# Layer 2's last row tiles multiplied from idle buffers, products five steps behind the scores, 16 dummy matmuls in place of 24

## The chip, the cores and the metric

One Trainium2 chip, one of its cores. The metric is device time of one launch in microseconds (us). Engines: PE (TensorE, matmuls), DVE (VectorE), ACT (ScalarE), POOL (GpSimd) and SP (SyncE, here the queue that issues every DMA).

## What is computed

Four graph-attention layers on x (16 batch elements, 1024 nodes, 64 features) with one adjacency matrix per element; each layer is followed by `x = layernorm(x + layer(x))`. Layer 2, whose end the change touches, has 8 heads:

```
scores = einsum('bmhd,bnhd->bhmn', q, k) * scale + edge_bias[edges]
scores = leaky_relu(scores, 0.2), masked where edges == 0
attn   = softmax(scores, axis=-1)
out    = einsum('bhmn,bnhd->bmhd', attn, v) @ Wp + bp
```

Layer 3 scores a pair of nodes by `a . leaky_relu(u_i + v_j)` over 64 features, then softmax, product and ELU.

## The kernel before

Each engine runs its own hand-written program; semaphores alone order them. The outer loop (`Fori`) has one turn per batch element g: layer 3 of element g, with layers 0 and 1 of element g+1 woven in (`ahead`), then layer 2 of element g+1. So there are 16 ends of layer 2; 15 of them are followed by a layer 3 that has the next element's work in it.

Layer 2 runs 4 pairs of heads x 8 row tiles = 32 steps `s`, two tiles `n = 2s, 2s+1` (one per head) a step, 64 tiles in all. For a tile, PE makes 128x1024 scores (`scores`), ACT applies a ReLU, DVE combines to the leaky ReLU and takes a minimum (`leaky`, L1243), ACT takes the exponential. The result must be transposed before it can be multiplied. For 15 of the 16 quads (a quad is 4 tiles, 2 steps, number `k`) DVE transposes 32x32 blocks within partitions (L1271) into one of two buffers `blocks`, and SP issues 16 DMAs (`move`, L380) that carry the blocks across partitions into one of three buffers `quadT`. `pv_quad(k, part)` (L697) then multiplies half a quad, `LAG = 3` quads behind the scores, so at steps 2k+6 and 2k+7. The last quad (tiles 60 to 63) isn't moved: PE transposes its tiles into PSUM (`turn`, L522) and DVE copies them out (L1276) into a `blocks` buffer, whose last content must have been moved first. Between these, PE also makes the next pair's queries (`q`), values (`vw`) and transposes the last pair's result (`heads`); all of these share the PSUM space `turn`, one at a time, in the order of `extra_use`. DVE multiplies a pair's turned heads by the inverse row sums (`pair_out`, L1284) and POOL adds them up.

When the last pair's products are done, ACT copies them (L959), PE turns them (`turn_heads`), and DVE, after its loop has closed, adds, normalises and writes `x2`. PE meanwhile closes its loop, makes two products for the next element (`first_products`, L527 and L544), issues `KEEP = 24` dummy matmuls (L776), then turns x2 and makes layer 3's columns and values. ACT makes `ucol` in two halves (L1021, L1022). Layer 3's main loop starts with the first matmul of L808. POOL converts the next element's adjacency rows from `adj_in` into `mask_next` during layer 2.

## Time and profile before

| | us |
|---|---|
| median of 3 runs | 9054.23 (9046.0 to 9068.25) |
| the profiled execution's own time | 9052.68 |
| its span | 9050.9 |
| PE, DVE, ACT, POOL busy | 90%, 82%, 78%, 16% of the span |
| mean granted TensorE clock | 0.958 of full |

Times in the rows are microseconds from the span's start. A row of the timeline merges like instructions that follow each other; in brackets stands the engine's idle time before them and what ended it. A clock of 1.00 is 2.4 GHz, 0.50 is 1.2 GHz. One turn of the loop takes some 553 us: the dummies of one end of layer 2 start at 3226.27, those of the next at 3780.78.

### The profile page before, as it was taken

The page shows a single profiled execution, that of the slowest core. Times are in us where ns is not written, and L with a number is a line of the kernel's source. Part 1 is how long each engine was busy: PE and PEld are TensorE (multiplying, and loading weights), DVE is VectorE, ACT ScalarE, POOL GpSimd, SP SyncE. Part 2 cuts the span into 40 slices and gives each one's busy share as a digit, 9 for nine tenths or more (in the row PEclk, how much of TensorE's full clock was granted, in tenths as well). Part 3 has the DMA queues.
Part 4 walks back from the last instruction along what each step waited for, and adds up shares of the span by engine and source line. Part 5 has one row for each costly group of instructions (what it writes and reads, how often), then busy time and mean ns, then how long its engine had stood idle before and what let it go on. Part 6 is the DMA issues. An engine that isn't in the chain of part 4 may idle for free.

```text
span 9050.9 us, 165102 instructions
## 1 busy us (share of the span) xinstructions
PE 8158.5 (90%) x57976; PEld 3621.5 (40%) x57976; DVE 7394.6 (82%) x11173; ACT 7034.4 (78%) x8220; POOL 1429.1 (16%) x582
## 2 busy tenths in 40 slices
PE   3899998989999899998998989899898998999999
PEld 1434435343353433434334353443534435343352
DVE  3788787987879878798787978878788787987878
ACT  2788786977869778787787878778688786977877
POOL 0301203021030301203012030120302103021000
PEclk7999999999999999999999999999999999999999
DMA  2715426253362623527145271542715426253251
GB/s 72 159 35 114 101 50 155 42 129 80 66 139 50 144 58 78 129 46 165 37 100 112 47 167 35 114 98 53 155 39 120 91 49 155 44 132 75 56 126 19
DMA packets 2150347, 822.58 MB, mean 91 GB/s; under 512 B 1146914, under 2 KB 2129954, under 8 KB 2147362
## 3 DMA queue, kind: packets, MB, share of 16 engines
q1 hardware_dynamic: 2149410, 810.76, 40.9%
q8 instruction: 507, 8.31, 0.4%
q14 instruction: 430, 3.52, 0.1%
HBM read 76.25 MB, written 4.19 MB: 9 GB/s over the span
## 4 chain that ended last, share of the span: by engine, by line
PE 36%; SPq 21%; DVE 18%; issue 13%; ACT 8%; DMA 3%; DVEq 0%; POOL 0%; ACTq 0%; POOLq 0%
SPq L380 20%; PE psum L808 19%; DVE work L1379 6%; ACT work L1035 5%; PE psum L527 3%; PE psum L697 3%; DVE work L1271 3%; DVE work L1243 3%; PE psum L599 2%; PE psum L522 2%; PE psum L544 1%; PE psum L776 1%; DMA work<-work 1%; PE psum L669 1%; ACT spare L877 1%
## 5 line engine op out<-in xcount | busy, mean ns | idle before, releaser
L808 PE MATMUL psum<-work,pick 128*32 128x512 f32 x32768 | 3758.0, 598 | 198.1 <-DVE work L1379 162.2
L1035 ACT ACTIVATE work<-spare,ucol 128x1024 f32<-128x1024 f32 x3402 | 3633.7, 1147 | 52.0 <-PE psum L808 48.6
L1379 DVE TENSOR_SCALAR work<-spare,ucol 128x1024 f32<-128x1024 f32 x4790 | 3250.2, 745 | 305.8 <-ACT ucol L1022 233.7
L808 PEld LDWEIGHTS psum<-work,pick 128*32 128x32 f32 x32768 | 975.9, 110 | 2532.0 <-issue 2065.5
L944 ACT ACTIVATE work<-psum,beta 128x1024 f32<-128x1024 f32 x1024 | 1138.9, 1112 | 474.0 <-PE psum L669 395.6
L1271 DVE STREAM_TRANSPOSE work<-work 128x1024 f32<-128x1024 f32 x960 | 1191.1, 1241 | 295.3 <-DMA work<-work 177.1
L1243 DVE CUSTOM_DVE_ANT_0 work<-psum,work 128x1024 f32<-128x1024 f32 x1024 | 1225.7, 1197 | 155.0 <-ACT work L944 143.6
L951 ACT ACTIVATE work<-work,least 128x1024 f32<-128x1024 f32 x1024 | 1172.2, 1145 | 54.7 <-DVE least L1243 54.5
L665 PE MATMUL psum<-mask,ident_b 128*128 128x512 bf16 x2048 | 643.5, 397 | 304.3 <-DVE least L1243 301.0
L1460 POOL TENSOR_TENSOR rstd<-rstd,neg_half 128x8 f32<-128x8 f32 x64 | 131.6, 2056 | 4951.5 <-DVE rstd L1182 4951.5
L669 PE MATMUL psum<-x_split,q_hi 128*128 128x512 f32 x2048 | 862.0, 503 | 0.0
L697 PE MATMUL psum<-work,vw 128*64 128x256 f32 x5632 | 701.7, 393 | 0.0
L669 PE MATMUL psum<-x_split,q_lo 128*128 128x512 f32 x2048 | 660.2, 404 | 0.0
L1438 POOL TENSOR_SCALAR mask_next<-adj_in 128x1024 bf16<-128x1024 int32 x120 | 436.4, 3637 | 442.8 <-DMA adj_in<-in_adj 434.7
L697 PEld LDWEIGHTS psum<-work,vw 128*64 128x64 f32 x5632 | 384.4, 140 | 285.6 <-issue 130.2
L669 PEld LDWEIGHTS psum<-x_split,q_hi 128*128 128x128 f32 x2048 | 405.1, 198 | 159.9 <-issue 15.5
L1440 POOL TENSOR_SCALAR no_edge<-adj_in 128x1024 bf16<-128x1024 int32 x120 | 436.1, 3634 | 9.5
L669 PEld LDWEIGHTS psum<-x_split,q_lo 128*128 128x128 f32 x2048 | 398.1, 194 | 92.3
L1146 DVE CUSTOM_DVE_ANT_0 spare<-psum,spare 128x1024 f32<-128x1024 f32 x256 | 311.2, 1216 | 110.5 <-ACT spare L872 107.3
L665 PEld LDWEIGHTS psum<-mask,ident_b 128*128 128x128 bf16 x2048 | 125.2, 99 | 688.3 <-DVE least L1243 524.0
L872 ACT ACTIVATE spare<-psum,sbias 128x1024 f32<-128x1024 f32 x256 | 284.4, 1111 | 91.2 <-PE psum L582 77.9
L599 PE MATMUL psum<-q_lo,vw 128*64 128x256 f32 x2048 | 262.9, 401 | 67.3 <-DMA q_lo<-spare 37.1
(161 smaller groups left out, 6985.1 us busy)
## 6 DMA issues: line engine op xcount, KB each, us to landing
work<-work SPq DMA_DIRECT2D x2560, 128.0 KB, 2.5
spare<-work SPq DMA_DIRECT2D x1280, 128.0 KB, 2.5
adj_in<-in_adj SPq DMA_DIRECT2D x128, 512.0 KB, 4.9
q_lo<-adj_in SPq DMA_DIRECT2D x1024, 64.0 KB, 2.1
q_lo<-spare SPq DMA_DIRECT2D x1024, 64.0 KB, 2.1
work<-work SPq DMA_DIRECT2D x1792, 32.0 KB, 1.9
mask<-mask_next SPq DMA_DIRECT2D x16, 2048.0 KB, 9.3
x_in<-in_x SPq DMA_DIRECT2D x16, 256.0 KB, 9.6
```

Source lines behind the costliest of these rows:

```text
L380: sp.dma_start(dst[32 * c:32 * c + 32, :, a, :], src[32 * a:32 * a + 32, :, c, :]).then_inc(done, 16)
L599: mm = pe.matmul(dst, values[layer][:, j, :], src[:, j, :, :, :], start=(j < 2), stop=(j >= NT - 2))
L665: pe.matmul(slot[:, cols], ident_b[:], mask[:, t, cols], start=True, stop=False)
L669: mm = pe.matmul(slot[:, cols], left, x_split[:, cols], start=False, stop=(k == 1))
L697: mm = pe.matmul(dst, vw[:, pair % 2, j, F * h:F * h + F], src[:, j, :, h, :].rearrange("p a (t i) -> p a t i", t=2), start=(j == 0), stop ...
L808: mm = pe.matmul(slot[32 * q:32 * q + 32, cols], pick[:, 15 - kk:47 - kk], ring[kk % 4][q][:, cols], start=False, stop=(kk == 15), skip_gr ...
L944: act.activation(probs[n % 4], score[n % 2], ACT.Relu, bias=beta4[:, t, 2 * pair + h:2 * pair + h + 1], scale=GAIN[2]).then_inc(s_relu, 1)
L951: act.activation(probs[n % 4], probs[n % 4], ACT.Exp, bias=least[:, n % 4:n % 4 + 1], scale=-1.0, accum_out=rowsum[:, pair % 2, 2 * t + h: ...
L1035: ins = act.activation(ring[kk % 4][q], v3, ACT.Relu, bias=ucol[:, 4 * T + q, kk:kk + 1])
L1243: dve.tensor_tensor_reduce(probs[n % 4], score[n % 2], probs[n % 4], -ALPHA[2], 3.0e38, ALU.add, ALU.min, least[:, n % 4:n % 4 + 1]).then_ ...
L1271: dve.transpose(dst[:, :, h, half, :], probs[n % 4].rearrange("p (b j) -> p b j", j=32))\
L1379: ins = dve.tensor_scalar(ring[kk % 4][q], v3, ucol[:, 4 * T + q, kk:kk + 1], 0.0, ALU.add, ALU.max)
```

## The change

Six edits, all around the end of layer 2:

1. The last four tiles go to two idle places instead of a `blocks` buffer: tiles 60 and 61 into `adj_in` (after POOL has converted the last adjacency rows), tiles 62 and 63 into the first half of a `quadT` buffer (after quad 12's products). They are multiplied one row tile at a time (`pv_last`), the first before quad 14, the second after it.
2. `LAG` becomes 5 steps: `pv_quad(k, part)` runs at steps 2k+5 and 2k+6, one step earlier. `heads` moves from t=7 to t=6, `vw` from t=6 to t=5, the copies of the heads from t=2 and 6 to t=1 and 5.
3. `KEEP` goes from 24 to 16 dummies.
4. DVE's last `pair_out` is taken out of the branch at the end of layer 2 and stands at the start of `layer3`, behind the loop's end.
5. DVE writes x2 before the next element's column correction (`column_low`), not after it.
6. DVE makes one half of `ucol`, ACT the other. The queue of POOL gets one semaphore increment for the last element.

```diff
-LAG = 3
+LAG = 5
-KEEP = 24
+KEEP = 16
...
+        last_rows = [adj_in[:].rearrange("p a b -> p (a b)").bitcast(F32),
+                     work[:, 4:6, :].rearrange("p a b -> p (a b)")]
...
+            def pv_last(it, half):
+                in_sbuf(pe, it, ("tile", TILES2 - 3 + 2 * half))
+                src = last_rows[half].rearrange("p (b a h i) -> p b a h i", a=4, h=2, i=32)
+                cols = slice((NT - 2 + half) * P, (NT - 1 + half) * P)
+                for j in range(NT):
+                    for h in range(2):
+                        mm = pe.matmul(outT[F * h:F * h + F, cols], vw[:, (HP - 1) % 2, j, F * h:F * h + F],
+                                       src[:, j, :, h, :], start=(j == 0), stop=(j == NT - 1))
...
-                    if s >= 2 * LAG:
-                        pv_quad(g, it, s // 2 - LAG, s % 2, tail)
+                    if s >= LAG:
+                        pv_quad(g, it, (s - LAG) // 2, (s - LAG) % 2, tail)
...
-                pv_quad(g, it, QUADS - 3, 1, tail)
-                for k in (QUADS - 2, QUADS - 1):
-                    pv_quad(g, it, k, 0, tail)
-                    pv_quad(g, it, k, 1, tail)
+                pv_quad(g, it, MOVED - 2, 0, tail)
+                turn_tile(g, it, TILES2 - 2)
+                pv_quad(g, it, MOVED - 2, 1, tail)
+                turn_tile(g, it, TILES2 - 1)
+                pv_last(it, 0)
+                pv_quad(g, it, MOVED - 1, 0, tail)
+                pv_quad(g, it, MOVED - 1, 1, tail)
+                pv_last(it, 1)
                 turn_heads(g, it, HP - 1)
...
+                if h == 0 and half == 0:
+                    dve.wait_ge(s_mask_next, g + 2)
+                if h == 0 and half == 1:
+                    dve.wait_ge(s_pv, g * QUADS + MOVED - 2)
...
-                pair_out(g, it, HP - 1)
```

PE at the end of layer 2, before. `ident,work` is a tile turned, `ident,heads_T` a pair's heads turned, `work,vw` and `spare,vw` products of a quad (x8 is half a quad):

```order
L697 MATMUL psum<-work,vw 64x4x2x32 x8
L522 MATMUL psum<-ident,work 128x128 x8
L665 MATMUL psum<-mask,ident_b 128x512 x2
L669 MATMUL psum<-x_split,q_hi 128x512 x2
L669 MATMUL psum<-x_split,q_lo 128x512 x2
L522 MATMUL psum<-ident,work 128x128 x8
L522 MATMUL psum<-ident,heads_T 128x128 x8
L697 MATMUL psum<-work,vw 64x4x2x32 x8
L522 MATMUL psum<-ident,work 128x128 x8
L697 MATMUL psum<-work,vw 64x4x2x32 x8
L522 MATMUL psum<-ident,work 128x128 x8
L697 MATMUL psum<-work,vw 64x4x2x32 x8
L697 MATMUL psum<-spare,vw 64x4x2x32 x16
L697 MATMUL psum<-work,vw 64x4x2x32 x16
L522 MATMUL psum<-ident,heads_T 128x128 x8
```

And PE there now:

```order
L523 MATMUL psum<-ident,heads_T 128x128 x8
L695 MATMUL psum<-work,vw 64x4x2x32 x8
L523 MATMUL psum<-ident,work 128x128 x8
L666 MATMUL psum<-mask,ident_b 128x512 x2
L670 MATMUL psum<-x_split,q_hi 128x512 x2
L670 MATMUL psum<-x_split,q_lo 128x512 x2
L523 MATMUL psum<-ident,work 128x128 x8
L695 MATMUL psum<-work,vw 64x4x2x32 x8
L523 MATMUL psum<-ident,work 128x128 x8
L695 MATMUL psum<-work,vw 64x4x2x32 x8
L523 MATMUL psum<-ident,work 128x128 x8
L708 MATMUL psum<-adj_in,vw 64x128 x16
L695 MATMUL psum<-spare,vw 64x4x2x32 x16
L708 MATMUL psum<-work,vw 64x128 x16
L523 MATMUL psum<-ident,heads_T 128x128 x8
```

The third pair's heads and the second half of quad 12 now stand ahead of the last scores, and half of the last quad's product stands ahead of quad 14's.

DVE from the last `leaky` to the loop's end and behind it, before:

```order
L1276 COPY work<-psum 128x32x32 [waits s_turned,s_quad_moved1]
L1243 ISA work,least<-psum,work 128x1024 [waits s_relu]
L1243 ISA least 128x1
L1276 COPY work<-psum 128x32x32 [waits s_turned]
L1280 RECIPROCAL rinv<-rowsum 128x16
L1284 TENSOR_TENSOR heads_T<-psum,rinv 128x1024 [waits s_turned,s_acc,s_vec]
L1276 COPY work<-psum 128x32x32 [waits s_turned] x2
L1280 RECIPROCAL rinv<-rowsum 128x16
L1284 TENSOR_TENSOR heads_T<-psum,rinv 128x1024 [waits s_turned,s_acc,s_vec]
L1326 UNCONDITIONAL_BRANCH
L1397 UNCONDITIONAL_BRANCH
```

And now:

```order
L1288 COPY adj_in<-psum 128x32x32 [waits s_turned,s_mask_next]
L1251 ISA work,least<-psum,work 128x1024 [waits s_relu]
L1251 ISA least 128x1
L1288 COPY adj_in<-psum 128x32x32 [waits s_turned]
L1288 COPY work<-psum 128x32x32 [waits s_turned,s_pv]
L1288 COPY work<-psum 128x32x32 [waits s_turned]
L1340 UNCONDITIONAL_BRANCH
L1418 UNCONDITIONAL_BRANCH
L1375 RECIPROCAL rinv<-rowsum 128x16
L1074 ISA
L1376 ISA [waits s_vec]
```

The wait for quad 13's move became waits for the mask and for a product, and the last multiplication stands behind both branches.

## Rows read from the trace of the kernel before

**Rows 1.** The page, part 4: chain that ended last, by engine, by line.
```profile
PE 36%; SPq 21%; DVE 18%; issue 13%; ACT 8%; DMA 3%; DVEq 0%; POOL 0%; ACTq 0%; POOLq 0%
SPq L380 20%; PE psum L808 19%; DVE work L1379 6%; ACT work L1035 5%; PE psum L527 3%; PE psum L697 3%; DVE work L1271 3%; DVE work L1243 3%; PE psum L599 2%; PE psum L522 2%; PE psum L544 1%; PE psum L776 1%; DMA work<-work 1%; PE psum L669 1%; ACT spare L877 1%
```

**Rows 2.** Groups of instructions, all stretches: busy, mean ns | idle, releasers.
```profile
L1271 DVE STREAM_TRANSPOSE work<-work 128x1024 f32<-128x1024 f32 x960 | 1191.1, 1241 | 295.3 <-DMA work<-work 177.1 <-DMA spare<-work 117.7
```

**Rows 3.** Timeline, PE, an end of layer 2: start us, us, engine line op.
```profile
3194.50 1.09 PE L522 MATMUL psum<-ident,work 128*128 128x128 f32 x8 [2.41 <-DVE work L1276]
3196.99 1.96 PE L522 MATMUL psum<-ident,heads_T 128*128 128x128 f32 x8 [1.39 <-DVE work L1276]
...
3207.03 3.62 PE L697 MATMUL psum<-spare,vw 128*64 128x256 f32 x32
3210.49 3.62 PE L697 MATMUL psum<-work,vw 128*64 128x256 f32 x32
3214.80 1.09 PE L522 MATMUL psum<-ident,heads_T 128*128 128x128 f32 x8 [0.70 <-ACT heads_T L959]
```

**Rows 4.** Timeline, SP, the same end: quad 14's 16 DMA issues.
```profile
3190.21 11.55 SPq L380 DMA_DIRECT2D spare<-work  x16
```

**Rows 5.** Line L380 from 3125 to 3206 us.
```profile
DMA to landing us min/median/max: 2.3/2.8/4.4
```

**Rows 6.** Timeline, SP and PE, the ends with the longest and shortest gap.
```profile
6519.04 10.51 SPq L380 DMA_DIRECT2D spare<-work  x16
...
6537.93 3.62 PE L697 MATMUL psum<-spare,vw 128*64 128x256 f32 x32
...
7637.22 11.64 SPq L380 DMA_DIRECT2D spare<-work  x16
...
7651.19 3.62 PE L697 MATMUL psum<-spare,vw 128*64 128x256 f32 x32
```

**Rows 7.** Timeline, PE, layer 3: products of 64 weights with 128 columns.
```profile
3323.08 1.09 PE L762 MATMUL psum<-work,vw 128*64 128x128 f32 x16
```

**Rows 8.** Timeline, DVE, around the same end.
```profile
3193.22 1.22 DVE L1276 COPY work<-psum 128x1024 f32<-128x1024 f32 x1 [2.35 <-DMA work<-work]
...
3219.19 1.42 DVE L1364 TENSOR_TENSOR za<-za,heads_T 128x512 f32<-128x512 f32 x2 [2.03 <-issue]
...
3225.38 0.76 DVE L1188 TENSOR_TENSOR x<-zb,rstd 128x256 f32<-128x256 f32 x2
3242.95 4.73 DVE L1379 TENSOR_SCALAR work<-spare,ucol 128x1024 f32<-128x1024 f32 x7 [16.80 <-ACT ucol L1022]
```

**Rows 9.** Timeline, POOL: the last mask rows of the next element.
```profile
3180.02 2.14 POOL L1443 TENSOR_TENSOR mask_next<-mask_next,no_edge 128x1024 bf16<-128x1024 bf16 x1
```

**Rows 10.** Timeline, PE, from the loop's end to layer 3's first matmuls.
```profile
3219.26 3.77 PE L527 MATMUL psum<-xT_in,WD 64*128 64x512 f32 x4 [3.36 <-issue]
...
3226.27 7.57 PE L776 MATMUL psum<-mask,ident_b 128*128 128x512 bf16 x24
3233.68 1.04 PE L522 MATMUL psum<-ident,x 128*64 128x128 f32 x8
...
3249.31 2.87 PE L808 MATMUL psum<-work,pick 128*32 128x512 f32 x16
```

**Rows 11.** The same at the next end of layer 2.
```profile
3787.43 1.04 PE L522 MATMUL psum<-ident,x 128*64 128x128 f32 x8
...
3798.05 1.92 PE L808 MATMUL psum<-work,pick 128*32 128x512 f32 x16 [0.54 <-ACT work L1035]
```

**Rows 12.** Stretches at the first end: busy of PE, PEld, DVE, ACT, POOL, granted clock, DMA.
```profile
3226.00:3230.00 4.00, 4.00 (x11) 1.50 (x11) 0.14 (x1) 0.67 (x2) 0.00 (x0) 0.50 0.00 0
3230.00:3234.00 4.00, 4.00 (x19) 1.91 (x18) 0.00 (x0) 0.00 (x0) 0.00 (x0) 0.90 0.00 0
```

**Rows 13.** One stretch behind x2's transposes at each of 15 ends: first and last.
```profile
478.00:483.00 5.00, 5.00 (x24) 2.99 (x23) 1.76 (x3) 3.91 (x5) 0.00 (x0) 1.00 0.00 0
...
8239.00:8244.00 5.00, 5.00 (x17) 3.45 (x16) 1.01 (x2) 1.67 (x3) 0.00 (x0) 0.50 0.00 0
```

More of the change, by code:

```diff
@@ L64, in extra_use @@
     pair, t = divmod(s, NT)
-    if t == 7 and pair:
+    if t == 6 and pair:
         return ("heads", pair - 1)
     if pair + 1 < HP:
-        return {3: ("q", 2 * pair + 2), 4: ("q", 2 * pair + 3), 6: ("vw", pair + 1)}.get(t)
+        return {3: ("q", 2 * pair + 2), 4: ("q", 2 * pair + 3), 5: ("vw", pair + 1)}.get(t)
     return None
@@ L712, in layer2 @@
                 scores(g, it, 1, tail)
-                for s in range(STEPS2):
-                    pair, t = divmod(s, NT)
+                for s in range(STEPS2 - 1):
                     n = 2 * s
-                    more = s + 1 < STEPS2
                     extra = extra_use(s)
-                    if more:
-                        scores(g, it, n + 2, tail)
+                    scores(g, it, n + 2, tail)
                     if extra:
@@ L985, in layer2 @@
                         elu3(tail)
-                    if t == 2 and pair:
+                    if t == 1 and pair:
                         copy_out(g, pair - 1, 0)
-                    if t == 6 and pair:
+                    if t == 5 and pair:
                         copy_out(g, pair - 1, 1)
@@ L1264, in turn_tile @@
                 k, half, h, moved = in_quad(n)
-                if k >= 2 and half == 0 and h == 0:
+                if moved and k >= 2 and half == 0 and h == 0:
                     dve.wait_ge(s_moved[(k - 2) % 4],
```

51 lines of the change are left out of this document (28 added, 23 removed).

## The prediction

> **What bounds the kernel now.** The chain of work that ended last has PE first and SP's queue second: L380, the DMA issues of layer 2's moves, is 20% of the span, and L808, layer 3's main loop, 19% [rows 1]. So two regimes alternate. In layer 2 the chain runs through SP: 16 issues take 11.6 us for a quad [rows 4], and DVE stood 295 us before its transposes, nearly all of it for a move to land [rows 2]. In layer 3 PE, ACT and DVE are all loaded. Between them, once per batch element, lies a stretch in which one engine at a time works, and the change is about that. The timeline of PE there shows it: the last tile transposes with waits of 2.41 and 1.39 us, quad 14's product at 3207.03, the last quad's at 3210.49, the heads at 3214.80 [rows 3], the loop's end 3.36 us, two products, 24 dummies in 7.57 us, x2's transposes at 3233.68 and the first matmul of layer 3 at 3249.31 [rows 10]. DVE has x2 ready at 3226.1 (3225.38 + 0.76) [rows 8], 7.5 us before PE turns it. From the heads to layer 3, PE is the chain and DVE waits.
>
> **Earlier start and shorter end of the last products.** Quad 14's last DMA is issued at about 3201.1 (3190.21 + 11.55 less one issue of 0.65) [rows 4] and lands some 2.8 us later [rows 5], say 3203.8. PE starts its product at 3207.03 [rows 3], 3.3 us late. The change takes from PE between tile 61's transposes and that product: the heads with their wait (1.39 + 1.89) and the second half of quad 12 (2.45, what lies between the heads and the next transposes), and adds the first `pv_last`. Its price is bounded by two rows: 16 records with 64 weights and 128 columns took 1.09 us [rows 7], it has 32, so 2.1 us at most without overlap; half a quad with as many columns is 1.8 (3.62 / 2) [rows 3]. I take 1.95. So 12.53 - 3.28 - 2.45 + 1.95 = 8.75 us behind 3194.50, PE is ready at 3203.3, about when the move lands. The start at 3194.50 itself should hold: the copy of tile 60 no longer waits 2.35 us for quad 13's move [rows 8], while the third pair's multiplication (1.2 us and a reciprocal of 0.24) now stands ahead of it. Behind quad 14's product stands 1.95 us of work in place of 3.5, so 1.5 us more.
>
> The gap between landing and product differs: taken the same way at all 16 ends it lies between 0.4 us (7651.19) and 6.4 us (6537.93) [rows 6], mean 3.5. I take off 0.5 for ends at which PE isn't ready at the landing. 3.5 - 0.5 + 1.5 = 4.5 us, x 16 = **72 us**. Bounds: 1.5 (24 us in all, if PE is never earlier) and 5.0 (80 us).
>
> The new waits are covered: the mask that tile 60's copy waits for was done at 3182.2 [rows 9], 11 us before that copy; behind the copy on DVE stand the last `leaky` and the other copies, so it would matter at once if POOL came later. The wait for quad 12's product is met, since that product now stands before tile 60's transposes on PE.
>
> **Products one step earlier in the loop.** A step is about 6 us (half of the 11.6 us of SP's issues for a quad [rows 4]), so every product starts that much sooner behind its move. I take the worse case, that this uses up the slack and PE waits for some landings, and cost it at nothing still: DVE waits in the same step for the same landing before its transposes [rows 2], and the scores that stand behind the product on PE need a `leaky` that stands behind a transpose of 1.24 us; transpose and `leaky` are 2.4 us, the half quad 1.9. SP's order and its DMAs don't change, POOL's queue gets its heads a step sooner and has time for them. Bounds: 0 and, in a rival below, a slip of each quad.
>
> **Dummies.** 24 take 7.57 us [rows 10]; the clock was 0.50 until 3230 and then full [rows 12], so some 9 run at 0.43 us each and 15 in the remaining 3.6, 0.21 to 0.24 each. Eight fewer at full clock are 1.7 us, and PE is the chain there, since x2 is ready long before: also in the change, where PE would come to the transposes at least 15 us behind the heads and DVE needs 10.2 (3215.9 to 3226.1). 16 x 1.7 = **27 us**. At half clock they would be 3.4 us each end; nothing if DVE were late.
>
> **What the clock does behind the dummies.** At 15 ends I asked for the granted clock in a stretch just behind x2's transposes: 8 have 1.00, 7 have 0.50 [rows 13]. Where it fell, x2's transposes to layer 3's first matmul took 15.6 us (3233.68 to 3249.31) and its first 16 records 2.87 [rows 10]; where it didn't, 10.6 us and 1.92 [rows 11]. A fall costs 5.0 + 0.95, about 6 us. PE has dense dummies, then 1.04 us of transposes, 1.2 us idle and dense products. In the end with a fall the clock had been full for 3.5 us when the dummies ended; with 8 fewer it is full for about 1.8 us. The sparse stretch then comes sooner behind the rise, with the products right behind it. No row shows this spacing. I estimate that 5 of the 7 falls go: 5 x 6 = **30 us**. Bounds: none goes (0), and all go (42 us), or 8 new ones come, below.
> The Trainium skill (TensorE: Matmul & The Clock Gate, part 4) says that transposes on PE don't count as busy for the clock; by it the sparse stretch is longer than the rows of PE suggest, and fewer dummies would be the wrong direction. The rows don't tell transposes from idle time.
>
> **What hangs on nothing.** Moving `pair_out` behind the loop's end takes away DVE's 2.03 us between multiplication and additions [rows 8], and x2 before the column correction another 1.2, but both end at x2, which waits for PE. Half of `ucol` on DVE starts DVE's ring tiles 0.7 us earlier than 3242.95 [rows 8], but PE's first ring matmul came at 3249.31 behind its own products, or 0.54 us behind ACT [rows 11], which must copy the values first. All three: 0.
>
> **Sum.** The profiled execution's own time is 9052.7, 1.5 us under the median. 9052.7 - 72 - 27 - 30 = **8924 us**, 1.4% faster.
>
> **The rivals.**
> - *The falls stay.* Fewer dummies shift them but as many remain: 9052.7 - 72 - 27 = 8954. For it: 7 of 15 is near a coin's toss, and what decides isn't visible in the rows.
> - *The last products stay late.* PE isn't ready at the landing, because the turned tiles go back and forth between PE and DVE and the third pair's heads now precede them: only 1.5 us of the 4.5. 9052.7 - 24 - 27 - 30 = 8972. Against it: the sum above, which has PE ready 0.5 us before the landing.
> - *Too few dummies to raise the clock.* It stays at half through transposes and products: 8 ends more pay 6 us (+48), 15 pay 0.9 in the transposes (+14), the dummies give nothing. 9052.7 - 72 + 62 = 9043, no difference. Against it: the clock rose some 4 us into the dummies [rows 12], and 16 at half clock last 6.8. The rule "transposes don't count" above would point here too.
> - *Products in the loop wait and hold the scores.* If each quad's blocks come w later because PE stood for a landing, SP starts later, and the chain is SP's: 15 quads x 16 x w = 240 w. With w = 1 it is 8924 + 240 = 9164; it decides from w = 0.54, and is slower by over 0.3% from 0.65. Against it: DVE waits for the same landings, and a late product only touches tiles three quads on.
> - *More than the sum.* All 7 falls go and PE is ready at every landing: 80 + 27 + 42 = 149, 8904; if PE, fed more evenly, also has fewer of its short falls inside layer 2, a little less: 8900.
>
> **How the numbers follow.** Forecast 8924: 0.48. Falls stay (8954): 0.20. Last products stay late (8972): 0.09. Clock stays at half (9043): 0.05. Loop slips: 0.08, of which 0.05 above 9081. Even faster (8900): 0.10. The range 8885 to 8980 takes in the forecast with its bounds (8903 with 80, 27 and 42), the even faster case and the first two rivals, and leaves out 0.13 and tails. About 0.3% (27 us) is what a measurement of this kernel can tell from no change. Faster by more: 0.87. Within it: 0.08. Slower by more: 0.05.
>
> **What would show it.** Right: quad 14's product within 1 us of its landing, heads some 6 us behind that landing, 16 dummies in 5 to 6 us with the clock rising among them, at most 3 of 15 stretches at 0.50, PE still waiting for nothing but "issue" at the loop's end. Wrong: PE waits before L695 for DMAs longer than DVE does before its transposes, a longer time from the first `leaky` to the last than now, or clocks of 0.50 in the products behind x2.

## The result: 0.6% faster, not 1.4%

Measured: 9010.28 us median of 5 runs (8996.97 to 9021.64) against 9061.8 of the kernel before on the same chip (5 runs, 9046.0 to 9070.84). The ratio is 0.9943, 95% interval 0.9926 to 0.9959. The forecast was 8924, its range 8885 to 8980: the direction was right, the time 86 us too low and outside the range. Of the 129 us forecast, 51.5 came. The profiled execution of the changed kernel took 9021.64 (span 9019.7), the slowest of the five.

Both traces were cut at the same points in all 16 turns and the stretches summed. "Loop" is from the first `leaky` of an element to the landing of quad 14, "late" from that landing to quad 14's product, and the last two stretches part at the end of the sixteenth matmul of layer 3's main loop. For the kernel before I give the same sums from its trace.

| Sum over 16 elements, us | before | after | difference | forecast |
|---|---|---|---|---|
| loop | 3181.6 | 3249.6 | +68.0 | 0 |
| late | 56.0 | 2.2 | -53.8 | -48 (3.0 x 16) |
| quad 14's product to heads | 124.5 | 99.5 | -25.0 | -24 (1.5 x 16) |
| heads to x2's transposes (dummies in it) | 272.8 | 244.8 | -28.0 | -27 |
| x2's transposes to layer 3's 16th matmul | 251.1 | 259.0 | +7.9 | -30 |
| rest of layer 3 and what is woven in | 4899.1 | 4899.9 | +0.8 | 0 |

With -1.0 ahead of the first element that is -31.2, the difference of the spans (rounding apart). Three of the terms came as forecast. Two did not: the loop, 68 us, and the falls of the granted clock behind x2's transposes, 38 us (+7.9 where -30 was forecast).

What the chain that ended last says now, page part 4, by engine and by line (answers [rows 1]):

```profile
PE 38%; SPq 23%; DVE 15%; issue 13%; ACT 9%; DMA 1%; DVEq 0%; POOL 0%; ACTq 0%; POOLq 0%
```

PE and SP's queue have each gained 2 points, DVE has lost 3 and DMA 2. Groups of instructions, all stretches (busy, mean ns | idle before them, releasers), for DVE's `leaky` and block transposes, then products of quads on PE:

```profile
L1251 DVE CUSTOM_DVE_ANT_0 work<-psum,work 128x1024 f32<-128x1024 f32 x1024 | 1227.0, 1198 | 247.1 <-ACT work L953 237.4
L1279 DVE STREAM_TRANSPOSE work<-work 128x1024 f32<-128x1024 f32 x960 | 1190.9, 1240 | 263.3 <-DMA work<-work 168.7
...
L695 PE MATMUL psum<-work,vw 128*64 128x256 f32 x5120 | 641.4, 394 | 21.0 <-DMA work<-work 20.8
...
L695 PE MATMUL psum<-spare,vw 128*64 128x256 f32 x2560 | 312.6, 389 | 66.5 <-DMA spare<-work 66.5
```

The transposes wait 263 us, 32 less than in [rows 2]. PE now waits 87 us for landings ahead of its products, where it waited for none before. But the row to look at is the first. `leaky` stood 155.0 us before, 143.6 of them behind ACT's ReLU, in this line of the page of the kernel before:

```profile
L1243 DVE CUSTOM_DVE_ANT_0 work<-psum,work 128x1024 f32<-128x1024 f32 x1024 | 1225.7, 1197 | 155.0 <-ACT work L944 143.6
```

Now it stands 247.1. These 92 us are DVE waiting for ACT's ReLU, which comes as late as its scores do.

**The end of layer 2 did what was forecast.** Timeline of PE, changed kernel, the same end as [rows 3] and [rows 10] (start us, us, engine, line; in brackets the idle time before and what ended it):

```profile
3195.40 1.97 PE L708 MATMUL psum<-adj_in,vw 128*64 128x128 f32 x32
3199.31 3.67 PE L695 MATMUL psum<-spare,vw 128*64 128x256 f32 x32 [1.94 <-DMA spare<-work]
3202.78 1.95 PE L708 MATMUL psum<-work,vw 128*64 128x128 f32 x32
3205.41 1.09 PE L523 MATMUL psum<-ident,heads_T 128*128 128x128 f32 x8 [0.69 <-ACT heads_T L968]
3209.79 3.77 PE L528 MATMUL psum<-xT_in,WD 64*128 64x512 f32 x4 [3.28 <-issue]
...
3216.80 4.99 PE L784 MATMUL psum<-mask,ident_b 128*128 128x512 bf16 x16
3221.63 1.04 PE L523 MATMUL psum<-ident,x 128*64 128x128 f32 x8
3223.86 4.64 PE L528 MATMUL psum<-xTa,G 65*128 65x512 f32 x8 [1.20 <-ACT xTa L1025]
3228.30 3.52 PE L545 MATMUL psum<-linT_s,xTa 65*128 65x64 f32 x16
...
3236.41 3.64 PE L817 MATMUL psum<-work,pick 128*32 128x512 f32 x16
```

PE waits 1.94 us for quad 14 to land and starts its product with the landing; the estimate for half of the last quad (1.95) is measured as 1.97 and 1.95. The heads come 6.1 us behind the product's start where they took 7.8 [rows 3], and 16 dummies last 4.99 us where 24 took 7.57. A landing still takes about as long as before, 2.4 us in the median where [rows 5] has 2.8; line L381 from 3120 to 3204 us:

```profile
DMA to landing us min/median/max: 2.3/2.4/4.1
```

DVE's rows at that end, timeline: a copy into an idle place, `pair_out`'s reciprocal behind the loop's end, x2, and the first ring tiles:

```profile
3186.36 1.23 DVE L1288 COPY adj_in<-psum 128x1024 f32<-128x1024 f32 x1
...
3198.78 0.25 DVE L1375 RECIPROCAL rinv<-rowsum 128x16 f32<-128x16 f32 x1 [2.05 <-issue]
...
3213.45 0.76 DVE L1196 TENSOR_TENSOR x<-zb,rstd 128x256 f32<-128x256 f32 x2 [1.55 <-POOL rstd L1481]
...
3229.53 4.73 DVE L1400 TENSOR_SCALAR work<-spare,ucol 128x1024 f32<-128x1024 f32 x7 [0.23 <-DVE ucol L1388]
```

The copy into `adj_in` has no wait where its counterpart in [rows 8] waited 2.35 us, and the wait for the mask is met: POOL's last mask row ended at 3176.4. x2 is ready at 3214.2, 7.4 us ahead of its transposes (3221.63). So 16 dummies still cover DVE, and PE is the chain.

**The loss is in the loop, once per element.** Times from an element's first `leaky`, medians of 14 elements, show where:

| | quad 1 | quad 2 | quad 3 | quad 7 | quad 14 |
|---|---|---|---|---|---|
| SP starts its DMAs, before | 29.0 | 44.2 | 56.3 | 104.7 | 187.0 |
| after | 29.0 | 48.9 | 60.4 | 108.1 | 191.0 |

Up to quad 1 the two are alike; quad 2 starts 4.7 us late, and what follows carries it without growing. Summed over all 16 elements, the time from quad 1's first DMA to quad 2's is 308.0 us after and 240.6 before. These 67.4 us are as much as the whole loop lost; its other parts differ by up to 11 us either way and cancel. In the element with no layer 3 beside it (the first) quad 2 starts 0.9 us later, and quad 14 1.3 us earlier.

Timeline of PE in the changed kernel, one of step 4's scores and step 5 of one element:

```profile
3025.07 0.60 PE L666 MATMUL psum<-mask,ident_b 128*128 128x512 bf16 x2
...
3030.61 0.60 PE L666 MATMUL psum<-mask,ident_b 128*128 128x512 bf16 x2 [4.02 <-DVE least L1251]
...
3032.06 3.62 PE L565 MATMUL psum<-Cv,xTa 65*128 65x128 f32 x16
3035.61 3.45 PE L695 MATMUL psum<-work,vw 128*64 128x256 f32 x16
3038.99 0.61 PE L666 MATMUL psum<-mask,ident_b 128*128 128x512 bf16 x2
```

L565 is `vw(1)`, the second pair's values, and L695 the first product, quad 0's. Both now fall into step 5. PE has just stood 4.02 us, because DVE normalises layer 3's result there. The stretches of the same time (us, then busy and count of PE, PEld, DVE, ACT, POOL, granted clock, DMA share, GB/s) show the clock behind that pause:

```profile
3026.00:3030.60 4.60, 0.59 (x3) 0.16 (x1) 4.20 (x22) 3.00 (x5) 2.03 (x2) 1.00 0.66 148
3030.60:3032.00 1.40, 1.39 (x6) 1.08 (x7) 1.40 (x2) 1.23 (x2) 1.32 (x2) 0.95 0.88 204
3032.00:3035.60 3.60, 3.60 (x17) 3.32 (x15) 3.60 (x6) 1.11 (x1) 3.60 (x1) 0.50 0.89 200
3035.60:3039.00 3.40, 3.40 (x18) 1.74 (x18) 2.46 (x4) 2.15 (x3) 3.32 (x1) 0.55 0.56 128
```

The clock falls to 1.2 GHz behind the pause, and the two products run at it: 3.62 and 3.45 us instead of 1.95 each. The next scores come 7 us later, and DVE runs dry:

```profile
3036.82 1.24 DVE L1279 STREAM_TRANSPOSE work<-work 128x1024 f32<-128x1024 f32 x1
3041.82 1.23 DVE L1251 CUSTOM_DVE_ANT_0 work<-psum,work 128x1024 f32<-128x1024 f32 x1 [3.76 <-ACT work L953]
```

In the kernel before, PE pauses 3.10 us at this place and the clock falls too, but step 5 has only scores to make at 1.2 GHz. Both pieces stand at step 6, at 2.4 GHz. The pause in the timeline of PE, then stretches (columns as above), then the two pieces:

```profile
3036.06 0.89 PE L665 MATMUL psum<-mask,ident_b 128*128 128x512 bf16 x2 [3.10 <-DVE least L1243]
```

```profile
3036.00:3042.00 6.00, 5.13 (x12) 2.92 (x12) 6.00 (x8) 3.48 (x5) 5.84 (x4) 0.52 0.86 196
...
3044.00:3048.00 4.00, 4.00 (x35) 2.97 (x34) 4.00 (x6) 3.42 (x5) 3.73 (x3) 1.00 0.18 41
```

```profile
3044.09 1.95 PE L564 MATMUL psum<-Cv,xTa 65*128 65x128 f32 x16
3045.96 1.95 PE L697 MATMUL psum<-work,vw 128*64 128x256 f32 x16
```

That the pause is what brings the clock down is not shown: no run shortened it or put dummies into it.

### The profile page after: what moved, and what is told of

The parts are those of the page before. It is cut to its first block, busy times and chain, and to the rows that moved or that the text cites. A ratio compares the mean times of both kernels' runs of the same rounds, so it can differ in the third digit from the quotient of the medians.

```text
span 9019.7 us, 165963 instructions
## 1 busy us (share of the span) xinstructions
PE 8145.7 (90%) x58360; PEld 3645.7 (40%) x58360; DVE 7407.4 (82%) x11189; ACT 7012.7 (78%) x8204; POOL 1428.7 (16%) x582
## 4 chain that ended last, share of the span: by engine, by line
PE 38%; SPq 23%; DVE 15%; issue 13%; ACT 9%; DMA 1%; DVEq 0%; POOL 0%; ACTq 0%; POOLq 0%
SPq L381 22%; PE psum L817 21%; DVE work L1400 6%; ACT work L1043 5%; PE psum L528 3%; PE psum L600 3%; PE psum L695 2%; DVE work L1279 2%; PE psum L670 1%; DVE work L1251 1%; PE psum L523 1%; PE psum L545 1%; ACT spare L886 1%; ACT spare L881 1%; PE psum L784 1%
## 5 line engine op out<-in xcount | busy, mean ns | idle before, releaser
L817 PE MATMUL psum<-work,pick 128*32 128x512 f32 x32768 | 3766.7, 599 | 192.1 <-DVE work L1400 161.5
L817 PEld LDWEIGHTS psum<-work,pick 128*32 128x32 f32 x32768 | 977.8, 110 | 2531.4 <-issue 2069.1
L1251 DVE CUSTOM_DVE_ANT_0 work<-psum,work 128x1024 f32<-128x1024 f32 x1024 | 1227.0, 1198 | 247.1 <-ACT work L953 237.4
L695 PE MATMUL psum<-work,vw 128*64 128x256 f32 x5120 | 641.4, 394 | 21.0 <-DMA work<-work 20.8
L695 PEld LDWEIGHTS psum<-work,vw 128*64 128x64 f32 x5120 | 348.0, 140 | 292.8 <-issue 114.1
L695 PE MATMUL psum<-spare,vw 128*64 128x256 f32 x2560 | 312.6, 389 | 66.5 <-DMA spare<-work 66.5
```

Of the source, the lines that this page charges most:

```text
L695: mm = pe.matmul(dst, vw[:, pair % 2, j, F * h:F * h + F], src[:, j, :, h, :].rearrange("p a (t i) -> p a t i", t=2), start=(j == 0), stop ...
L817: mm = pe.matmul(slot[32 * q:32 * q + 32, cols], pick[:, 15 - kk:47 - kk], ring[kk % 4][q][:, cols], start=False, stop=(kk == 15), skip_gr ...
L1251: dve.tensor_tensor_reduce(probs[n % 4], score[n % 2], probs[n % 4], -ALPHA[2], 3.0e38, ALU.add, ALU.min, least[:, n % 4:n % 4 + 1]).then_ ...
```

## The experiments

The theory is that the loop loses because `vw(1)` and quad 0's product stand in the one step where PE comes out of a pause at 1.2 GHz. Its rivals are that the products, being earlier, wait for landings in every quad, or that the tail or DVE's edits do it. For the second miss the question is whether the falls stayed, moved or were paid elsewhere. All kernels had the kernel before run beside them on their chip; every difference below is the median's to that one. The sums are those of the first table, one trace for each kernel. The kernel before had medians of 9061.8, 9076.45 (beside e1 to e4), 9062.34 (e5 to e8) and 9081.5 (e9 to e12), so a difference of a few us between sums of different traces can be the chip's.

| | kernel | median | difference | ratio and interval | loop | late | product to x2's transposes | to 16th matmul |
|---|---|---|---|---|---|---|---|---|
| | before (first trace) | | | | 3181.6 | 56.0 | 397.3 | 251.1 |
| | after | 9010.28 | -51.5 | 0.9943, 0.9926 to 0.9959 | 3249.6 | 2.2 | 344.3 | 259.0 |
| e1 | after, `vw(1)` at step 6 | 8970.74 | -105.7 | 0.9878, 0.9857 to 0.9898 | 3197.1 | 3.0 | 354.2 | 249.5 |
| e2 | before, products a step earlier | 9044.30 | -32.2 | 0.9965, 0.9951 to 0.998 | 3220.9 | 2.2 | 412.5 | 256.1 |
| e3 | after, 24 dummies | 9044.37 | -32.1 | 0.996, 0.9943 to 0.9977 | 3245.1 | 3.1 | 379.7 | 257.6 |
| e4 | after, DVE's edits undone | 9016.27 | -60.2 | 0.9935, 0.9918 to 0.9952 | 3237.9 | 2.8 | 350.0 | 252.9 |
| e5 | after, products at the old steps | 8989.61 | -72.7 | 0.9918, 0.9901 to 0.9935 | 3173.2 | 53.7 | 344.7 | 248.2 |
| e6 | before, 16 dummies | 9003.36 | -59.0 | 0.9933, 0.9916 to 0.995 | 3190.1 | 27.3 | 375.5 | 234.1 |
| e7 | e1 with 5 dummies behind x2's transposes | 8942.69 | -119.7 | 0.9866, 0.9846 to 0.9887 | 3195.6 | 2.5 | 344.9 | 232.6 |
| e8 | e1 with 8 dummies | 8957.16 | -105.2 | 0.9885, 0.9866 to 0.9904 | 3181.1 | 2.4 | 315.0 | 273.4 |
| e9 | e5 with `vw(1)` at step 5 | 9018.30 | -63.2 | 0.9933, 0.9916 to 0.9949 | 3208.4 | 53.2 | 346.5 | 252.8 |
| e10 | before with 5 behind | 9035.55 | -46.0 | 0.9955, 0.9938 to 0.9972 | 3186.6 | 39.6 | 400.3 | 223.9 |
| e11 | e1 with 8 dummies, 5 behind | 8913.27 | -168.2 | 0.9827, 0.9809 to 0.9844 | 3189.4 | 2.5 | 319.3 | 222.8 |
| e12 | e1 with 8 dummies, 10 behind | 8917.60 | -163.9 | 0.9823, 0.9807 to 0.984 | 3189.1 | 2.2 | 315.9 | 233.2 |

**e1: one number in the table of steps.**

```diff
-        return {3: ("q", 2 * pair + 2), 4: ("q", 2 * pair + 3), 5: ("vw", pair + 1)}.get(t)
+        return {3: ("q", 2 * pair + 2), 4: ("q", 2 * pair + 3), 5 if pair else 6: ("vw", pair + 1)}.get(t)
```

> The changed kernel with one thing put back: in the first pair of heads, PE makes the next pair's values (vw) at step 6 again instead of step 5. Theory A (the loop lost 61.6 us over 16 elements because at step 5 of an element PE has vw and the first half quad's product in a row, straight behind the wait for DVE's layer-3 normalisation, so that the scores behind them come late): quad 2's first DMA comes back from 48.9 to about 44.5 us behind the element's first leaky, the loop's 16 stretches fall from 3111 to about 3050 us, and the time is 50 to 60 us less than the change, near 8955. Rival B (the products one step earlier wait for landings in every quad, and the values have nothing to do with it): quad 2 stays near 49, the time stays within 15 us of the change, 8995 to 9025.

The loop's sum falls by 52.5 us, the time by about 54 (105.7 less 51.5), and quad 2's DMAs start at 45.4. Products five steps behind stay as they are, so landings in every quad are not the cause of these 54 us. PE at step 5 and 6 in this kernel, timeline:

```profile
3018.12 0.61 PE L666 MATMUL psum<-mask,ident_b 128*128 128x512 bf16 x2 [4.03 <-DVE least L1251]
...
3019.70 3.46 PE L695 MATMUL psum<-work,vw 128*64 128x256 f32 x16
...
3025.85 1.95 PE L565 MATMUL psum<-Cv,xTa 65*128 65x128 f32 x16
3027.72 1.95 PE L695 MATMUL psum<-work,vw 128*64 128x256 f32 x16
```

The pause and the product at 1.2 GHz are still there. `vw(1)`, one step later, takes 1.95.

**e5: the tail without the earlier products.**

```diff
-LAG = 5
+LAG = 6
-    if t == 6 and pair:
+    if t == 7 and pair:
...
-        return {3: ("q", 2 * pair + 2), 4: ("q", 2 * pair + 3), 5: ("vw", pair + 1)}.get(t)
+        return {3: ("q", 2 * pair + 2), 4: ("q", 2 * pair + 3), 6: ("vw", pair + 1)}.get(t)
...
+                turn_heads(g, it, HP - 2)
+                pv_quad(g, it, MOVED - 3, 1, tail)
+                turn_tile(g, it, TILES2 - 2)
                 pv_quad(g, it, MOVED - 2, 0, tail)
-                turn_tile(g, it, TILES2 - 2)
...
```

> The kernel before's loop (products six steps behind, vw at step 6, heads at step 7) with the change's end of layer 2, its 16 dummies and DVE's part; the third pair's heads and the second half of quad 12 stay behind the last scores. The run of the loop's part alone had brought quad 14's product to its landing already (2.2 us of lateness in 16 ends, before 56) and cost 49 us in the loop. So, theory D: most of the 54 us that quad 14's product came earlier is the loop's edit, not the idle buffers. Then here the loop's stretches are about 3050 us, quad 14's product stays 30 us or more late in sum, the heads follow it 6.2 us later, and the time lies near the step-6 run or up to 20 us above it, ratio to before 0.988 to 0.991. Rival E: the idle buffers alone (no wait for quad 13's move) bring quad 14's product to its landing; then lateness is under 10 us and the ratio is 0.985 to 0.988.

It is 72.7 us faster than before. The whole change has 51.5; the intervals overlap (0.9901 to 0.9935, 0.9926 to 0.9959), so that the change without its earlier products is the faster is likely and not shown. The loop's loss is gone (3173.2, 76 under after), quad 2's DMAs start at 44.4, and quad 14's product is late again by 53.7. So the earlier start of quad 14's product and the loop's loss both belong to the earlier products, and the 53 us ahead of x2's transposes to the tail and the dummies.

**e9: `vw(1)` alone at step 5**, the edit against e5. With e1 and e5 this completes a table of two by two. Its columns differ in more than the first product: all products, the heads and the heads' copies are a step earlier on the right, and the third pair's heads and half of quad 12 stand ahead of the last scores there.

```diff
-        return {3: ("q", 2 * pair + 2), 4: ("q", 2 * pair + 3), 6: ("vw", pair + 1)}.get(t)
+        return {3: ("q", 2 * pair + 2), 4: ("q", 2 * pair + 3), 6 if pair else 5: ("vw", pair + 1)}.get(t)
```

> Tail-only kernel (products six steps behind, `heads` and `vw` of before) with one move: the second pair's values, `vw(1)`, at step 5 in place of 6. The fourth cell of a table: vw at 6 with products at 6 (8989.6), vw at 6 with products at 5 (e1, loop sum 3058.9), both at 5 (after, 3111.2). Theory A, each piece of PE work at step 5 delays quad 2 by its own length (1.95 us at full clock, more at half): 15 elements x 1.9 to 2.5 = 29 to 38 us, about 9022, loop sum about 3055. Rival B, only the pair of them in a row overruns DVE's slack: 8990. Rival C, the values alone do all of it: some 9040, quad 2's issues start 4.5 us later as in after.

| loop; start of quad 2's DMAs | products from step 6 | products from step 5 |
|---|---|---|
| `vw(1)` at 6 | 3173.2; 44.4 (e5) | 3197.1; 45.4 (e1) |
| `vw(1)` at 5 | 3208.4; 46.8 (e9) | 3249.6; 48.9 (after) |

By these sums `vw(1)` alone costs 35 us, the products alone 24, both together 76. But they run to quad 14's landing and hold the end of layer 2 as well, and they scatter: e6 and e10 have the loop of the upper left cell and measure 3190.1 and 3186.6; e7, e8, e11 and e12 have that of the upper right one and lie between 3181.1 and 3195.6. Cut at the place itself, the cells hardly scatter:

| from quad 1's first DMA to quad 2's, summed over 16 elements | products from step 6 | products from step 5 |
|---|---|---|
| `vw(1)` at 6 | 240.6 to 241.6 (before, e5, e6, e10) | 250.7 to 254.8 (e1, e7, e8, e11, e12) |
| `vw(1)` at 5 | 273.2 (e9) | 292.4 to 308.0 (after, e2, e3, e4) |

There the product alone costs 9 to 14 us, `vw(1)` alone 32, both 51 to 67, more than their sum. That would follow if DVE had slack in step 5 that is used up only once, which no run tests by itself. Theory A, that each piece costs its own length, holds in the trace for `vw(1)`: the loop up to the last `leaky`, the sum meant in the expectation, is 3056.9 where e5 has 3023.6. In the times it is not so plain: e9 is 29 us above e5 as measured, but only 9.5 when each is taken against the kernel before on its own chip, and their intervals overlap (0.9901 to 0.9935, 0.9916 to 0.9949). So the lone `vw(1)` rests on the trace, and the move of e1, 54 us, on times too.

The clock's part can be read inside the four traces that have both at step 5. In 14 of their 60 elements behind the first, the clock fell later: `vw(1)` took 2.06 to 2.83 us, and quad 2 started 17.2 to 17.5 us behind quad 1. In the other 46 it took 3.61 or 3.62, and quad 2 started 18.8 to 20.7 behind. The kernel before has 15.0 to 15.4. In the medians (19.8, 17.5 and 15.3) 2.3 of the 4.5 us go with the clock being down already when `vw(1)` starts. How much of the other 2.2 the clock has through the product behind is not separated.

`vw(1)` on PE and the next wait of DVE in e9, timelines:

```profile
3045.91 3.62 PE L565 MATMUL psum<-Cv,xTa 65*128 65x128 f32 x16
```

```profile
3053.35 1.23 DVE L1253 CUSTOM_DVE_ANT_0 work<-psum,work 128x1024 f32<-128x1024 f32 x1 [2.52 <-ACT work L955]
```

`vw(1)` took 3.62 us in 13 of the 14 middle elements here and in 13 of after, and 1.95 in all 14 of before, e1 and e5.

**e2: the kernel before with products a step earlier, and nothing else.**

```diff
-LAG = 3
+LAG = 5
...
-                    if s >= 2 * LAG:
-                        pv_quad(g, it, s // 2 - LAG, s % 2, tail)
+                    if s >= LAG:
+                        pv_quad(g, it, (s - LAG) // 2, (s - LAG) % 2, tail)
...
-                        pv_quad(g, it, QUADS - 3, 0, tail)
+                        pv_quad(g, it, QUADS - 3, 1, tail)
...
-                pv_quad(g, it, QUADS - 3, 1, tail)
```

with `heads`, `vw` and the copies moved as in the change.

> The kernel before with the loop's part of the change alone: products five steps behind, vw at step 5, heads at step 6, copies of heads one step earlier; the end of layer 2, the 24 dummies and DVE's part as before. Theories A and B both say slower than before by about 60 us (9115 to 9130), since the loop's stretches grow from 3050 to about 3110 us. If the change's loop is only slow together with its end of layer 2 (rival C), this is as fast as before, within 15 us.

I had it slower, and it is 32 us faster. The loop does lose (+39 in the trace), but with the third pair's heads and the second half of quad 12 ahead of the last scores, quad 14's product already starts at its landing: late 2.2 instead of 56. I had credited that gain to the new order of the tail. e5, which has the new tail and the old lag, is late by 53.7. So the earlier start of quad 14's product comes with the lag alone (and what moves with it), not with the tail.

Being early has a price of its own, which the change hardly pays. PE now waits for the landing, and behind that wait the clock can be down. PE at an end of e2, timeline:

```profile
3224.90 5.36 PE L697 MATMUL psum<-spare,vw 128*64 128x256 f32 x32 [2.79 <-DMA spare<-work]
```

The granted clock is 1.00 from 3221 to 3223 and 0.50 from 3225 to 3227, and the product takes 5.36 us instead of 3.62. In e2 that happened at 10 of 16 ends: product to heads sums to 141.5 us instead of 124.5, so 17 of the 54 are given back. In the traces that have the changed tail too it happened at 1 to 4 ends (after: 1), in those with a late product at none.

The profiled execution was the slowest of its seven, 19 us over the median, so its sums lie high.

**e4: DVE's three edits undone** (`pair_out` back in the branch, `column_low` ahead of x2, both halves of `ucol` on ACT).

```diff
+                pair_out(g, it, HP - 1)
...
-                dve.tensor_scalar(ucol[F:P, :, :], score[0].rearrange("p (a b) -> p a b", b=32)[F:P, :, 16:32],
-                                  mag[F:P, 0:1], None, ALU.mult).then_inc(s_ucol_dve, 1)
```

> The changed kernel with DVE's three edits undone: the last pair's multiplication back inside the branch ahead of the loop's end, x2 behind the column correction, both halves of ucol on ACT. My prediction costs all three at nothing: within 10 us of the change, and x2's transposes on PE still start right behind the last dummy. Rival: one of them is what shortened the end of layer 2, since 16 dummies end sooner and x2 is late without them; then PE waits for DVE before x2's transposes and this is 20 to 40 us slower than the change.

The intervals of e4 and after lie over each other (0.9918 to 0.9952, 0.9926 to 0.9959): the edits are worth nothing that can be measured. DVE's wait for `ucol`, 233.7 us over the run of the kernel before and 203.9 in e4, is 3.5 in after, and it bought nothing that the times show.

**e3 and e6: the dummies, in both kernels.**

```diff
-KEEP = 16
+KEEP = 24
```

> The changed kernel with 24 dummies. By the term of my sum (8 dummies at full clock, 1.7 us each of 16 ends, falls of the clock the same) it is 27 us slower than the change, near 9037. If the fall of the clock behind x2's transposes depends on the dummies as I had thought (fewer falls with 16), it is 27 + up to 30 slower, near 9065. In the change's trace the falls behind the dummies are as many as before (long ones at 6 of 15 ends, short ones at the others), so I now expect 20 to 35 us.

```diff
-KEEP = 24
+KEEP = 16
```

> The kernel before with 16 dummies, nothing else. My term says 27 us less (1.7 us at each of 16 ends) and falls of the clock 30 us less; from the run with 24 dummies in the change (114.5 us of dummies against 84.5, and the way from x2's transposes to layer 3 8 us longer) I now expect 25 to 40 us less, ratio 0.9955 to 0.9975. If the dummies' number shifted the falls as I had forecast it would be 0.9935 to 0.9945.

With 24 in after, the stretch up to x2's transposes grows by 35 us in the traces (the dummies alone by 27). The medians, against before, differ by 19. In the kernel before, the edit alone gives 59 us, more than the 25 to 40 expected and as much as the whole change (the intervals overlap). Of that its trace shows 22 ahead of x2's transposes, 17 behind them and 29 in "late", where nothing was edited; the loop was 8 longer. "Late" lies at 56.0, 39.6 and 27.3 in the three traces with the old lag and tail (before, e10, e6), so part of what a single trace shows there is chance, and the 53.8 of the first table lies at the high end.

**What the clock does behind the dummies.** The time from x2's transposes to the end of the sixteenth matmul of layer 3 takes only a few values. "Early" is a fall that lengthens already the first product behind the transposes (3.67 us at full clock), "late" one that comes behind that product. Counts of the 15 ends that have a next element:

| | no fall, 12.6 us | late fall, 13.5 to 16.1 us | early fall, 18.4 us and more |
|---|---|---|---|
| before, 24 dummies | 7 | 1 | 7 |
| e2, 24 | 7 | 0 | 8 |
| e3, 24 | 7 | 0 | 8 |
| after, 16 | 0 | 9 | 6 |
| e1, 16 | 0 | 11 | 4 |
| e6, 16 | 2 | 11 | 2 |
| e4, 16 | 1 | 9 | 5 |
| e5, 16 | 2 | 9 | 4 |
| e9, 16 | 0 | 10 | 5 |
| e8, 8 | 6 | 0 | 9 |
| e10, 24 and 5 behind | 7 | 8 | 0 |
| e7, 16 and 5 behind | 1 | 14 | 0 |
| e11, 8 and 5 behind | 9 | 6 | 0 |
| e12, 8 and 10 behind | 8, at 14.1 to 14.5 us | 7, at 14.3 to 15.5 us | 0 |

In e12 the ten behind lengthen every end, so time doesn't tell there: at 8 ends the transposes ran at half clock (1.81 to 1.92 us) and the products behind them at full. With 24 dummies an end has, but for one, either no fall or an early one, as [rows 13] showed. With 16, hardly an end has none. In place of it comes a late fall, in layer 3's first matmuls, which costs 1.0 to 2.6 us. After at the next end, stretches with the same columns as above, and PE there:

```profile
3778.00:3782.00 4.00, 2.80 (x13) 1.56 (x11) 0.00 (x0) 1.05 (x2) 0.00 (x0) 1.00 0.02 4
3782.00:3789.00 7.00, 7.00 (x26) 3.27 (x24) 5.09 (x8) 5.16 (x6) 0.00 (x0) 0.80 0.00 0
```

```profile
3779.97 3.67 PE L528 MATMUL psum<-xTa,G 65*128 65x512 f32 x8 [1.20 <-ACT xTa L1025]
3783.48 1.89 PE L545 MATMUL psum<-linT_s,xTa 65*128 65x64 f32 x16
3785.30 2.92 PE L528 MATMUL psum<-spare,lin 64*128 64x512 f32 x4
...
3789.12 3.64 PE L817 MATMUL psum<-work,pick 128*32 128x512 f32 x16
```

The first products are at full clock, from L528's 2.92 on (four matmuls; 3.78 with the clock at half) it is halved, and the sixteen of L817 take 3.64 where [rows 11] has 1.92. The early kind is the timeline shown above: clock 0.80 from 3224 to 3228, products of 4.64 and 3.52. In after, fewer dummies did not take the falls away. They moved them, and 7.9 us more were paid. In the kernel before (e6) they left 2 early falls of 7 and brought 11 late ones, and 17.0 us less were paid. What brings a late fall is open: e7 and e10 have 14 and 8 of them with the gap behind the transposes filled.

**e8: 8 dummies.**

```diff
-KEEP = 16
+KEEP = 8
```

> The step-6 kernel with 8 dummies. PE would come to x2's transposes some 12 us behind the heads, DVE has x2 after about 8 to 10. If the clock rises among them as before: 8 x 0.21 to 0.43 us x 16 = 27 to 50 us less. If 8 are too few and the clock stays at half through transposes and products (the rival that ended without a gain in my prediction): the way from the transposes to layer 3's first matmul is 15 to 17 us at nearly all ends, 60 us more, and the sum is 10 to 40 us slower than the step-6 run.

Against e1, 39 us go ahead of x2's transposes and 24 come back behind them: 9 early falls, each 6.7 us or more instead of 5.9, because at 8 of the 9 the transposes run at half clock too (1.84 to 1.91 us where 1.04 was the rule). In the medians against before, e8 and e1 are the same.

**e10: five dummies behind x2's transposes, in the kernel before.** PE waits there 1.20 us for ACT's copy in any case.

```diff
                 turned(turn_rows(lambda t: x2[:, t, :], F))
+                for i in range(5):
+                    pe.matmul(outT[:, 0:HALF], ident_b[:], mask[:, 0, 0:HALF], start=True, stop=True)
                 in_sbuf(pe, it, ("xT2", 0))
```

> The kernel before (24 dummies) with 5 dummies added between x2's transposes and the products behind them. Theory A, the clock falls because PE is sparse from x2's transposes to layer 3's first products: the 7 stretches of 15 us become 11 to 11.6, the sum from x2's transposes to layer 3 goes from 209.5 to about 182, minus 27 us, layer 3 unchanged: some 9033. Rival B, the falls only move into layer 3's first products or ahead of the transposes: 9062 or a little slower (5 x 0.21 x 16 = 17 us, 9079).

The early falls are gone, all 7, and 27 us with them (251.1 to 223.9); x2's transposes to layer 3's first matmul sum to 182.1. The span of the trace is 28.6 us lower, with 16 less in "late", where nothing was edited, and 12 more in the loop and layer 3. The median is 46 lower on its chip, so some 20 us of it are not accounted for. PE in the kernel with the filler, timeline:

```profile
3236.55 1.04 PE L522 MATMUL psum<-ident,x 128*64 128x128 f32 x8
3237.43 1.24 PE L780 MATMUL psum<-mask,ident_b 128*128 128x512 bf16 x5
3238.79 3.67 PE L527 MATMUL psum<-xTa,G 65*128 65x512 f32 x8
```

The 1.24 us fill the gap of 1.20 and cost nothing: from the transposes' start to the product it is 2.24 us here, and 2.23 in the timeline of after (3221.63 to 3223.86). This settles that PE's thinness right behind x2's transposes is what causes the early falls: filled, it leaves none here, in e7, e11 and e12. Whether the transposes or the idle time count there is still open, since every run here has both together.

The Trainium skill (TensorE: Matmul & The Clock Gate, part 4) says that the full clock doesn't engage for PE's transposes, which don't count as busy in the same way. What it says agrees with e10 in direction, and doesn't tell the late falls of 16 dummies from none with 24. The transposes here do run at either level, 1.04 or 1.91 us, as the clock stands when they begin. And "fewer dummies would be the wrong direction", which the prediction drew from it, is not borne out: 16 in place of 24 made the stretch 7.9 us longer in after and 17.0 shorter in e6.

**e7, e11 and e12: the filler with fewer dummies.** e7 is e1 with those 5, e11 has 8 dummies ahead as well, e12 has 8 ahead and 10 behind.

> The step-6 kernel with 5 more dummies, placed behind x2's transposes where PE stands 1.2 us for ACT's copy. Theory: the fall of the clock in the products that follow comes from that sparse stretch (transposes, then idle); if it is filled, the long falls (6 of 15 ends in the step-6 run, 14.9 us instead of 10.7 from the transposes to layer 3's first matmul) are gone, 20 to 35 us less than the step-6 run. Rival: the fall is decided by transposes and products themselves, or the dummies delay the products by more than they save: same or up to 15 us slower.

> After with vw(1) at step 6, 8 dummies ahead of x2's transposes and 5 behind them. With 8 ahead alone 10 of 16 stretches took 16 us instead of 10.7 (sum 228.2). Theory A, what kept the clock down there was the sparse stretch, and 5 behind it are enough: the sum goes to about 181, minus 40 to 47 us, some 8915. Rival B, with 8 ahead the clock has not risen when the transposes come, and 5 more are too few to raise it: no gain, 8957 to 8970.

> The same with 10 behind the transposes. Theory A: 5 more dummies at full clock cost 5 x 0.21 x 16 = 17 us over the kernel with 5 and bring nothing, some 8932. Rival B, where 5 were too few: 10 raise the clock, the long stretches go and this is the faster of the two, some 8935 against 8957 to 8970.

All three have no early fall. e7 is 119.7 us under before and spends 17 us less than e1 behind x2's transposes (20 to 35 were expected); in the medians against before it is 14 ahead of e1, and the intervals overlap. e11 is 168.2 us under before, 1.7%, the lowest median of all. Its ratio over that of after, 0.9827 / 0.9943 = 0.988, makes it 1.2% faster than the change as made, each taken against the kernel before on its own chip. Timeline of PE in e11:

```profile
3185.05 3.60 PE L784 MATMUL psum<-mask,ident_b 128*128 128x512 bf16 x8
3188.44 1.91 PE L523 MATMUL psum<-ident,x 128*64 128x128 f32 x8
3190.15 1.52 PE L788 MATMUL psum<-mask,ident_b 128*128 128x512 bf16 x5
3191.55 3.67 PE L528 MATMUL psum<-xTa,G 65*128 65x512 f32 x8
3195.06 1.90 PE L545 MATMUL psum<-linT_s,xTa 65*128 65x64 f32 x16
```

The transposes are at half clock, and the clock rises during the five behind them; L528 and L545 then take 3.67 and 1.90, full speed. So the rival, that 5 more would be too few to raise the clock, fell. e12's five more cost 10 us behind x2's transposes in the trace, as expected in size (17 at most), but the medians of e11 and e12 are the same within their intervals.

## Why the prediction was wrong where it was

- **Last products earlier, 72 us: right in size, wrong in cause.** Late -53.8 and product to heads -25.0 make 78.8. PE is at the landing at every end (2.2 us in all), and the single-tile product is 1.95 to 1.97. But e2 and e5 show that the first part comes with the lag, by which the heads and half of quad 12 stand ahead of the last scores, and with the tail's new order only the second. With "late" between 27 and 56 in traces of unchanged code and 2.2 now, 25 to 54 is what can be claimed for the first part.
- **Dummies, 27 us: right.** The trace has 28.0, with x2 ready 7.4 us ahead. That the rise would fall among 16 is right too (0.50 from 3213 to 3219, 0.89 from there to 3221.6).
- **Loop, "I cost it at nothing still": the step that failed first, 68 us.** The argument weighed the products against landings and against DVE's waits in the middle of the loop, and of what moves with them it priced only the products. `vw`'s move from step 6 to step 5 stood in the change and got no price of its own. Its place was the one to look at: in the trace of the kernel before, PE pauses at step 4 to 5 for DVE's normalisation, and the next stretch (3036 to 3042 us) has the clock at 0.52. Two pieces of work that were 1.95 us at step 6 would be 3.6 there, with DVE's slack of one transposition and one `leaky` behind them. Worked out afterwards, 15 x (3.6 + 3.5 - 2.4) = 70 us. That sum fits the pair alone: the same working gives 1.2 us an element for `vw(1)` by itself, and e9 shows 2.1 (32 over 15 elements). One of the prediction's own signs of being wrong came true: from the first `leaky` to the last it is 3111.2 us now, 3049.6 before. The rival that named the loop had the wrong mechanism: it let each of 15 quads slip by w, with PE waiting for landings. PE does wait 87 us for landings now, and DVE's transposes wait 32 less; that costs nothing, as forecast, since from quad 3's first DMA to quad 14's the sum is 2074.8 us now and 2085.2 before. What costs is one slip of some 4 us per element.
- **Falls of the clock, "I estimate that 5 of the 7 falls go": the second step that failed, +7.9 us where -30 was forecast.** The estimate saw two outcomes, a fall or none, and there are three. With 16 dummies hardly an end is left without a fall: after has 9 late falls of 1.0 to 2.6 us, beside 6 early ones of 5.9. The rival "the falls stay" (8954) had the early ones right; it and the loop's 68 give 9022, the profiled execution's 9021.64; the two small misses, -6.8 in the products and +7.9 here, cancel. In the kernel before, the same edit left only 2 early falls (e6): there 5 of 7 did go, and late falls took back part of the 30. What decides between 2 and 6 of them with 16 dummies is open: each kernel has one trace, and its runs lie 9 to 51 us apart.
- **DVE's edits, 0: right** (e4).
- **The chances.** 0.08 for the loop was too little for a move that put two pieces of work in a row on the engine that stands ahead of DVE. The range left its price out.

## What to carry to other kernels

Price every item that moves at its new place, not only the one that the change is about: what stands ahead of it, how long that engine has just paused, and at which granted clock the next stretch ran. The same 16 matmuls were 1.95 us at step 6 and 3.62 at step 5. When a change to one section brings a gain and a loss in two places, build the two-by-two table; here one number in a table of steps gave back 54 us.

Where PE is thin between dense work (transposes, then a wait for a copy), put throwaway matmuls into the wait itself and not ahead of it. Five in a gap of 1.20 us took away every early fall, which 8, 16 and 24 ahead of the transposes did not, and they let the 24 become 8. They did not take away the late ones.

## What the runs showed of the hardware that I had not expected

- Behind a pause of 4.02 us on PE the clock went down only after the work behind it had begun: granted clock 1.00 from 3026 to 3030.6, 0.95 to 3032, 0.50 from there to 3035.6.
- The kind of fall went with the number of dummies: with 24 and nothing behind the transposes there was no fall or one of 5.9 us (one end of 45 had 1.0), with 16 nearly always one, of 1.0 to 2.6 or of 5.9, with 8 again none or one of 6.7 and more.
- Behind a wait of 2.79 us for a landing the clock was 0.50, and 32 matmuls took 5.36 us instead of 3.62 (e2, 10 of 16 ends). The length of the wait alone doesn't decide: 3.0 us at another end of e2, and 1.94 at the end of after shown above, left it at full.
- PE was busy without a gap from 3209.79 on in after, first with fp32 products of 3.77 and 3.51 us and then with the dummies, and the clock stayed at 0.50 until 3219.
- With 8 dummies ahead and 5 behind the transposes the clock still rose in time at all 15 ends (none over 16.1 us), though the same 8 without the 5 left 9 ends at 19.3 us and more.
